# Layer 1's rotation in a two-layer transformer kernel: one sine product over 128 partitions, the halves exchanged by DMAs, additions some rows later

## What is computed

```python
def rope(x):                                  # x: head, token, 128 features
    x2 = x.reshape(*x.shape[:-1], 64, 2)
    rot = jnp.stack([-x2[..., 1], x2[..., 0]], axis=-1).reshape(x.shape)
    return x * cos + rot * sin
q, k, v = xn @ Wq, xn @ Wk, xn @ Wv           # split into heads
q, k = rope(q), rope(k)
scores = (q @ k.T + alibi) / sqrt(128)
scores = 30 * tanh(scores / 30)
probs = softmax(where(causal, scores, -inf))
out = concat_heads(probs @ v) @ Wo + bo
```

## Time and profile before

| | |
|---|---|
| runs | 869.60, 869.14, 864.97 us; median 869.14 |
| the profiled execution | 866.74 us, its span 865.0 us |
| busy | TensorE 779.7 us, VectorE 612.7, ScalarE 465.6, POOL 422.8 |
| layer 1's attention | from about 330 to 706 us of the span |
| DMA | 59.81 MB, most of it on SP's queue |

### The profile page before, as it was taken

How to read it: one execution, slowest core, us unless ns; L and a number is a source line. 1 busy time by engine, 2 the same in 40 slices (tenths; PEclk the granted TensorE clock), 3 DMA queues, 4 the chain that set the end, 5 groups by cost and what they waited for, 6 DMA issues and landing times.

```text
span 865.0 us, 13854 instructions
## 1 busy us (share of the span) xinstructions
PE 779.7 (90%) x4835; PEld 635.0 (73%) x4835; DVE 612.7 (71%) x1063; ACT 465.6 (54%) x819; POOL 422.8 (49%) x478
## 2 busy tenths in 40 slices
PE   2999999988788758898999899999999999999996
PEld 2876776764223237687988788989999999988884
DVE  8388869547988868788877886767766654445555
ACT  3433342259888823676645556556566555655431
POOL 2566846423554454454433357577663412665430
PEclk9999999998989988999999999999999999999999
DMA  5111186000000040000000001110110569644107
GB/s 180 38 53 57 38 243 179 1 1 1 1 1 2 1 143 6 26 7 7 25 7 13 7 26 50 44 37 32 56 50 1 197 128 346 218 146 106 48 4 241
DMA packets 50115, 59.81 MB, mean 69 GB/s; under 512 B 13559, under 2 KB 41084, under 8 KB 50048
## 3 DMA queue, kind: packets, MB, share of 16 engines
q1 hardware_dynamic: 45488, 50.49, 19.2%
q0 software_dynamic: 4560, 8.44, 2.7%
HBM read 41.11 MB, written 21.86 MB: 73 GB/s over the span
## 4 chain that ended last, share of the span: by engine, by line
PE 56%; DVE 12%; POOL 6%; ACT 6%; issue 4%; DMA 1%; POOLq 0%; ACTq 0%; DVEq 0%; SPq 0%
PE ps L771 12%; PE ps L515 8%; PE ps L517 7%; PE ps L516 7%; PE ps L864 4%; PE ps L861 3%; PE ps L895 3%; POOL A L1735 2%; DVE cap L1442 2%; DVE swap L1432 2%; PE ps L609 2%; PE ps L554 2%; PE ps L843 2%; PE ps L686 2%; PE ps L780 1%
## 5 line engine op out<-in xcount | busy, mean ns | idle before, releaser
L1105 ACT ACTIVATE cap<-cap 128x1024 f32<-128x1024 f32 (+7 forms) x128 | 87.1, 680 | 123.1 <-DVE cap L1442 123.1
L771 PE MATMUL ps<-V,P 128*128 128x129 f32 x1152 | 152.6, 279 | 0.0
L771 PEld LDWEIGHTS ps<-V,P 128*128 128x128 f32 x1152 | 145.2, 194 | 2.7
L1442 DVE SCALAR_TENSOR_TENSOR cap<-dist,ps 128x1024 f32<-128x1024 f32 (+7 forms) x128 | 95.1, 749 | 26.2 <-PE ps L517 21.4
L1661 POOL TENSOR_SCALAR_AFFINE_SELECT P<-P 128x128 f32<-128x128 f32 x128 | 38.6, 301 | 148.8 <-ACT P L1110 148.5
L1791 POOL DMA_INDIRECT y_scratch<-y_sb,aux_s x63 | 62.0, 984 | 61.6 <-ACT y_sb L1150 40.3
L1110 ACT ACTIVATE P<-cap 128x1024 f32<-128x1024 f32 (+7 forms) x128 | 87.7, 685 | 4.1
L515 PE MATMUL ps<-q_hi,k_hi 128*128 128x512 f32 x192 | 72.1, 376 | 6.9 <-DVE cap L1442 6.2
L517 PE MATMUL ps<-q_lo,k_hi 128*128 128x512 f32 x192 | 67.0, 349 | 0.0
L516 PE MATMUL ps<-q_hi,k_lo 128*128 128x512 f32 x192 | 66.8, 348 | 0.0
L1766 POOL TENSOR_TENSOR rot<-rot,swap 128x512 f32<-128x512 f32 x40 | 52.1, 1304 | 19.7 <-DVE swap L1432 19.5
(11 more groups left out here) (288 smaller groups left out, 2099.2 us busy)
## 6 DMA issues: line engine op xcount, KB each, us to landing
xg_scratch<-blank SPq DMA_DIRECT2D x1, 8127.0 KB, 32.5
xa<-xg_scratch SPq DMA_DIRECT2D x63, 128.0 KB, 2.2
ew<-in_experts SPq DMA_DIRECT2D x3, 1920.0 KB, 8.7
y<-y_scratch SPq DMA_DIRECT2D x8, 512.0 KB, 5.4
pk<-in_packed SPq DMA_DIRECT2D x8, 384.0 KB, 3.2
pks<-in_scales SPq DMA_DIRECT2D x8, 384.0 KB, 4.0
ew<-in_experts SPq DMA_DIRECT2D x1, 3072.0 KB, 12.9
wqk<-in_wqk SPq DMA_DIRECT2D x20, 128.0 KB, 2.0
```

What stands on the lines that cost most here:

```text
L771: last = pe.matmul(ps[:, 4 + r % 2, o:o + D1 + 1], P1[:, h % 2, a:a + P], V1[:, j, h // REP, :], start=(j == 0), stop=(j == t))
L1105: act.activation(cap[:, n % 2, 0:w], cap[:, n % 2, 0:w], ACT.Tanh, scale=1.0 / (CAP * float(D1) ** 0.5))\
L1442: dve.scalar_tensor_tensor(out=cap[:, n % 2, 0:w], in0=dist[:, 0:w], scalar=slope, in1=psf[:, 1024 * (n % 2):1024 * (n % 2) + w], op0=ALU. ...
```

## The change

VectorE multiplies the whole bank with the sine in one instruction over 128 partitions, into a new tile sines with one buffer. SP copies its two halves crosswise into swap by two DMAs within SBUF; the semaphores swapped0 and swapped1 count them. A product waits until the exchange before it has read sines; POOL's addition waits for the exchange. In VectorE's program the wait for pj_rot is gone; SP waits for it instead. Outside the start, POOL's addition now comes one row after the projection's row, ScalarE's copy (with the split of wqk) two rows and POOL's subtraction three rows after it. SP loads wqk a projection earlier, between the exchanges, and wo has one buffer. One semaphore (table_ready) is folded into another.

```diff
+        sines = sb("sines", [P, HALF])
...
-        wo = sb("wo", [P, 2, PAIR, D])
+        wo = sb("wo", [P, PAIR, D])
...
+            def load_wqk(n):
+                if n < len(PROJ):
                     sp.wait_ge(wqk_ready, n - 1)
                     sp.dma_start(wqk[:, n % 2], wqk_in[n]).then_inc(in_wqk[n % 2], 16)
+
+            def load_wo(m):
+                if m >= 1:
+                    sp.wait_ge(wo_ready, m)
...
+            def exchange(i):
+
+                sp.wait_ge(pj_cos, i + 1)
+                if i >= 2:
+                    sp.wait_ge(pj_rot, i - 1)
+                for to, frm in ((slice(0, 64), slice(64, 128)), (slice(64, 128), slice(0, 64))):
+                    sp.dma_start(swap[to, i % 2, :], sines[frm, :]).then_inc(swapped[i % 2], 16)
+
+            load_wqk(2)
+            for n, (kind, i) in enumerate(PROJ):
+                exchange(2 * n)
+                exchange(2 * n + 1)
+                load_wqk(n + 3)
                 if kind == "q" and i % PAIR == 0 and i >= PAIR:
                     load_wo(i // PAIR - 1)
...
-                if i >= 2:
-                    dve.wait_ge(pj_rot, i - 1)
                 dve.tensor_tensor(rot[:, k % 3], b, cos1[:, tk], ALU.mult)
-                for to, frm in ((slice(0, 64), slice(64, 128)), (slice(64, 128), slice(0, 64))):
-                    last = dve.tensor_tensor(swap[to, i % 2, :], b[frm, :], sin1[frm, tk], ALU.mult)
-                last.then_inc(pj_cos, 1)
+                if i >= 1:
+                    dve.wait_ge(swapped[(i - 1) % 2], 32 * ((i - 1) // 2 + 1))
+                dve.tensor_tensor(sines[:], b, sin1[:, tk], ALU.mult).then_inc(pj_cos, 1)
...
                 pool.wait_ge(pj_cos, i + 1)
+                pool.wait_ge(swapped[i % 2], 32 * (i // 2 + 1))
                 pool.tensor_tensor(r, r, swap[:, i % 2, :], ALU.add).then_inc(pj_rot, 1)
...
+    rows_later = {"act": (0, 2), "dve": (0, 0), "pool": (1, 3)}[engine]
...
+            now = n < first_row or engine == "dve"
+            out += [x for _, x in todo if now]
+            pending += [x for x in todo if not now]
```

More of the change, by code:

```diff
@@ L361, in build_program @@
         in_pk, in_l1c = [sem("in_pk0"), sem("in_pk1")], sem("in_l1c")
-        in_wqk, in_wo, in_wv = [sem("in_wqk0"), sem("in_wqk1")], [sem("in_wo0"), sem("in_wo1")], sem("in_wv")
+        in_wqk, in_wo, in_wv = [sem("in_wqk0"), sem("in_wqk1")], sem("in_wo"), sem("in_wv")
         in_router = sem("in_router")
@@ L401, in build_program @@
         fT_ready, f_ps, fth_ready, x_ready = sem("fT_ready"), sem("f_ps"), sem("fth_ready"), sem("x_ready")
-        table_ready = sem("table_ready")
+        swapped = [sem("swapped0"), sem("swapped1")]
         mixed, shift_ready = sem("mixed"), sem("shift_ready")
@@ L466, in load_rows @@
                 sp.dma_start(rows_of(b), xg_dram[b * P:(b + 1) * P, 0:D]).then_inc(in_xg[b % NT], 16)
[L468 to L475, removed]
+            def load_wqk(n):
+                if n < len(PROJ):
                     sp.wait_ge(wqk_ready, n - 1)
                     sp.dma_start(wqk[:, n % 2], wqk_in[n]).then_inc(in_wqk[n % 2], 16)
+            def load_wo(m):
+                if m >= 1:
+                    sp.wait_ge(wo_ready, m)
+                sp.dma_start(wo[:], wo_in[m * PAIR * D1:(m + 1) * PAIR * D1, :].rearrange("(h p) n -> p h n", p=P))\
+                    .then_inc(in_wo, 16)
+            def exchange(i):
[9 more added lines that the diff above has]
+                load_wqk(n + 3)
                 if kind == "q" and i % PAIR == 0 and i >= PAIR:
@@ L974, in _ @@
             act.wait_ge(consts_ready, 1)
-            act.activation(ln_sd[:, 0:1], consts[:, 0:1], ACT.Sqrt).then_inc(table_ready, 1)
-            act.wait_ge(table_ready, 1)
+            act.activation(ln_sd[:, 0:1], consts[:, 0:1], ACT.Sqrt).then_inc(act_step, 1)
+            act.wait_ge(act_step, 1)
             act.wait_ge(in_const, 32)
@@ L1084, in split_wo @@
             def split_wo(m):
-                act.wait_ge(in_wo[m % 2], 16 * (m // 2 + 1))
+                act.wait_ge(in_wo, 16 * (m + 1))
                 if m >= 1:
                     act.wait_ge(s_ps, NT * m)
-                act.activation(wo_hi[:], wo[:, m % 2], ACT.Copy).then_inc(wo_hi_ready, 1)
+                act.activation(wo_hi[:], wo[:], ACT.Copy).then_inc(wo_hi_ready, 1)
             def project_part(n, half):
@@ L1106, in scores @@
                     .then_inc(act_step, 1)
-                act.wait_ge(act_step, n + 1)
+                act.wait_ge(act_step, n + 2)
                 if j == 0 and h >= 2:
@@ L1758, in split_wo @@
                 pool.wait_ge(wo_hi_ready, m + 1)
-                pool.tensor_tensor(wo_lo[:], wo[:, m % 2], wo_hi[:].bitcast(F32), ALU.subtract).then_inc(wo_ready, 1)
+                pool.tensor_tensor(wo_lo[:], wo[:], wo_hi[:].bitcast(F32), ALU.subtract).then_inc(wo_ready, 1)
             def project(n, half):
@@ L1863, in follow @@
 def follow(engine):
-    out, later = [], []
+    out, later, pending = [], [], []
+    first_row = next(n for n, s in enumerate(STEPS1) if s[0] == "scores")
+    rows_later = {"act": (0, 2), "dve": (0, 0), "pool": (1, 3)}[engine]
     for n, s in enumerate(STEPS1):
@@ L1873, in follow @@
             out.append(s)
+            pending = [(rows - 1, x) for rows, x in pending]
+            out += [x for rows, x in pending if rows <= 0]
+            pending = [(rows, x) for rows, x in pending if rows > 0]
             if engine in ROUTER and NT * s[1] + s[2] in ROUTER[engine]:
@@ L1888, in follow @@
         elif name == "project":
+            todo = []
             if engine != "act":
-                out.append(s)
+                todo.append((rows_later[0], s))
             if engine != "dve":
-                later.append(("project_part", *s[1:]))
+                todo.append((rows_later[1], ("project_part", *s[1:])))
                 if s[2] == 1 and s[1] + 2 < len(PROJ):
-                    later.append(("split_wqk", s[1] + 2))
+                    todo.append((rows_later[1], ("split_wqk", s[1] + 2)))
+            now = n < first_row or engine == "dve"
+            out += [x for _, x in todo if now]
+            pending += [x for x in todo if not now]
         elif name == "moe":
```

## The result

| | before | after |
|---|---|---|
| median of the runs (8 each) | 868.18 us | 875.24 us (872.04 to 879.75) |
| ratio | 1 | **1.0092**, 95% interval 1.0065 to 1.0118 |
| the profiled execution, its span | 866.74, 865.0 us | 876.26, 874.5 us |
| layer 1's attention: transpositions of its input to the first score row / from there to head 15's | 23.2 / 341.8 us | 26.5 / 346.7 us |

The change makes the kernel slower by 0.9%, 7 us; the prediction said 860, and its range ended at 875. Nearly all of it lies in the attention: 3.3 us at its start and 4.9 us in its heads. The heads that lose most, from first score row to first score row, are 10 (27.6 us for 24.8), 2 (27.8 for 25.6) and 0 (17.4 for 16.0); head 10 has no stall of VectorE at all.

What follows compares the result with a forecast made beforehand. TensorE bounds the kernel, held up by pauses behind VectorE in layer 1's attention, heads 0 to 9. Saved 11.2, less 2.2, 0.8 and 1.0, makes 7.2 us off 866.74: 859.5, given as 860, whole range 849 to 875.

Steps and rivals of the forecast that it cites:

- What goes: VectorE's rotation: 40 sine products on 128 partitions replace 80 on 64, taking away 27.5 us of its work.
- What is saved: Layer 1's attention, heads 0 to 9: 11.2 us in all after stalls, including 2.4 in heads 7 and 9.
- 0.69 us a projection, up to the excess: Early heads: each projection saves 0.69 us, less stalls, at most the head's excess over its length without pauses.
- The 2.4 us for heads 7 and 9: Pauses of 0.70 and 1.70 us go, as ScalarE's copy comes a row later, behind the next tanh and exponential.
- (1) The stalls: VectorE, one sines buffer: waiting for the 2.8 us exchange stalls it 1.1 us where behind, 0.4 where TensorE paces it.
- (2) The start: Before the first score row: exchanges lengthen POOL's rounds, +2.2 us, plus 0.8 for an even chance of slow clock.
- (3) The late low parts: Ends of heads 2, 6 and 10: POOL's subtraction, three rows behind, comes late, about 0.4 us each, 1.0 in all.
- What cost nothing: Single wo buffer free; last wo load delays the expert loads some 5 us, still 20 us before the attention ends.
- Slower, through the exchange: Rival, chance 0.17: exchange takes 4.4 us, start +8.3, stalls some 1 us a head in heads 0 to 5; 878 us.
- All of it comes back: Rival, chance 0.13: exchange at its low end, VectorE never stalls in the attention; 16 us off, 850.
- A wash: Rival, chance 0.22: exchange takes 3.4 us, stalls of 1.7, 4.3 lost at the start; under 2 off, 865 us.
- What would have shown it wrong: Signs: sines waiting over 1.5 us a time, first scores after 353, TensorE waiting for q_lo at over three heads' starts.

Runs made afterwards that it cites:

- e11: The change with first four products made without DMA, POOL's subtraction two rows behind, second sines buffer overwriting part of x_tok: 860.79 us, 0.9906 of the kernel before.
- e8: The change with the first four products made without DMA and POOL's subtraction two rows behind instead of three: 869.71 us, 1.0033 of the kernel before.
- e12: The change with first four products without DMA, subtraction two rows behind, second sines buffer in s_tok until product 14, nothing overwritten: 862.63 us, 0.9946 of before.
- e3: The change with only the first four products, before the first score row, made as before without DMA: 874.96 us, 1.0069 of the kernel before.
- e4: The kernel before with one sine product of 128 partitions straight into swap, halves not exchanged, old order kept: 0.993 of the kernel before.
- e2: The kernel before with only the change's later order of ScalarE's and POOL's parts, two sine products, no exchange: 1.0137 of the kernel before.
- e1: The change with the old order of ScalarE's and POOL's parts, exchange by DMA kept: 1.0101 of the kernel before.
- e5: The change with POOL's subtraction two rows behind its projection instead of three: 1.0097 of the kernel before.
- e6: The change with a second sines buffer, laid over part of the residual x_tok, which it overwrites: 870.32 us, 1.0037 of the kernel before.

## Why the prediction was wrong

**What goes: right.** 27.5 us of VectorE's work were to go; the group went from 55.1 to 27.4.

**The sum, term by term.** The prediction nets the stalls out of its 11.2 us. Taken apart (an estimate: 0.69 us a product in heads 0, 1, 2, 3 and 5, less what it counts there), they are 4.7 us, and the saving ahead of them 15.9. The runs' column is in shares of 868 us; it takes the rungs in the ladder's order, rounded one by one.

| term | forecast | in the runs |
|---|---|---|
| saved, before stalls | -15.9 | -8.2 (e11) |
| stalls at the one sines buffer | +4.7 | +11.0 (e11 to e8; the 7.6 from e12 to e8 are clear of the intervals, the rest is not) |
| late low parts | +1.0 | +3.1 (e8 to e3) |
| the start, slow clock included | +3.0 | +2.0 (e3 to after) |
| together | -7.2 | +8.0 |

So the two steps that failed are the saving, 7.7 us too large, and the price of the stalls, 6.3 too small; the late parts come third, with 2.1.

**What is saved: too large.** The run without exchange and without stalls (e4) shortens all heads by 341.8 - 334.5 = 7.3 us and heads 0 to 6 by 5.3, where the prediction had 8.8 in heads 0 to 6 even after its stalls. The step that failed is "0.69 us a projection, up to the excess". It holds in head 2, where e4 saves the forecast 1.1 us and 3.07 us of the longest pause stay, and fails in heads 1, 4 and 6: after its stalls the forecast has 2.3 (slow clock included), 1.5 and 2.0 there, and e4 saves 0.8, 0.1 and 0.4. In head 6 TensorE waits for VectorE's additions to s_tok, and three products of 128 partitions for six don't shorten that: 0.58 and 2.09 us before, 0.93 and 1.75 in e4.

```profile
491.15 0.39 PE L515 MATMUL ps<-wo_hi,cT_hi 128*128 128x256 f32 x1 [0.58 <-DVE s_tok L1471]
...
502.57 0.38 PE L515 MATMUL ps<-wo_hi,cT_hi 128*128 128x256 f32 x1 [2.09 <-DVE s_tok L1471]
```

```profile
485.39 0.38 PE L515 MATMUL ps<-wo_hi,cT_hi 128*128 128x256 f32 x1 [0.93 <-DVE s_tok L1469]
...
496.44 0.38 PE L515 MATMUL ps<-wo_hi,cT_hi 128*128 128x256 f32 x1 [1.75 <-DVE s_tok L1469]
```

The prediction took the whole difference between a head and its length without pauses as VectorE's rotation work coming late. Why head 4 gives only 0.1 isn't taken apart.

The 2.4 us for heads 7 and 9 came in half. Both pauses are gone, and head 7 takes 19.0 us for 20.0, but head 9 takes 22.7 for 22.6: at its end VectorE waits 2.97 us for the sends (587.08), and TensorE 1.59 for VectorE (until 588.74). The prediction asked what ended the pause, and not what would end next: the last send lands where it did in the head before, and VectorE, some 2 us earlier, can't go on without it.

**(1) The stalls: the size nearly right, the price too low.** The exchange is 2.9 us where 2.8 was taken, and of the eleven stalls within the heads nine have 0.39 to 0.90 us, about the forecast 0.4 to 1.1. Two, in heads 1 and 2, have 2.06 and 1.84, since those exchanges took 4.6 and 4.3 us. The 11 stalls make 9.8 us; with the second buffer until head 4 (e12) they fall from e8's 9.9 to 3.7, 6.2 us less, and the heads get 343.7 - 335.3 = 8.4 us shorter (7.6 by the ratios). All of it lies in heads 0 to 3. So once the low parts are in time a stall of VectorE there costs about all that it takes; whether more is within what single profiles differ by. How is argued, not tried apart: the score row is queued behind it, and tanh, the exponential and POOL's mask behind that, and the slow clock after a pause adds to it.

**(2) The start: right.** +2.2 us was forecast, +3.3 measured (26.5 against 23.2), and the first score's matmul waits 2.66 us for q_lo, as the chain said. But 0.8 of the 3.3 us lie ahead of the first product, where the programs do the same: the first cosine product starts 5.43 us behind the first transposition before and 6.27 after, with the granted clock at its low level in after. The windows of before and of after, from the first projection on:

```profile
330.20:332.50 2.30, 2.30 (x11) 1.80 (x10) 1.88 (x5) 0.63 (x2) 0.00 (x0) 0.85 0.00 0
```

```profile
332.00:334.30 2.30, 2.30 (x8) 1.82 (x7) 1.60 (x4) 0.60 (x1) 0.00 (x0) 0.50 0.00 0
```

From that cosine product to the first score row it is 17.79 us before and 20.19 after, **+2.4**: 2.2 until POOL's first addition, and 0.2 in the rounds. In the seven other kernels that start with two products (e2, e3, e8 to e12) it is 17.78 to 17.81, and in e1, e5 and e6, which start as the change does, 19.89 to 20.86.

**(3) The late low parts: 1.0 us forecast, 3.1 by the ladder.** "About 0.4 each, 1.0 us in all", in heads 2, 6 and 10. There are five waits, 8.2 us (10.8 less the start's 2.66), at the ends of heads 0, 1, 2, 6 and 10. The prediction priced one subtraction by its own delay behind one mask. But in POOL's queue the moved additions and subtractions stand behind one another, behind the split of wqk and of wo and, in head 10, the sends; and in head 2 they wait together for a mask whose score row is late on VectorE, behind the router's run and a stall of 1.84 us (403.43). The order alone shows them in e2: 8.3 us in four waits behind the start's, and 1.4% of time. By the ladder only 3.1 of the 8.2 us are time lost; without these waits TensorE waits 5.3 us more for VectorE's cap (e5).

**What cost nothing: right.** The first load of experts is issued at 698.20 us for 679.41, so 18.8 us later, where "some 5" was said (10 of them are the attention's own lateness). From head 15's first score row to the end of the span it is 172.8 us, before 173.2.

**The clock.** The granted clock from 350 to 400 us is 0.93 as before, at more pauses; in the 4 us from 424 on, behind the wait at 422.04, it is 0.67 (windows of after), which is the low level, 1.2 GHz, for two thirds of them. The 0.8 us allowed for the start didn't come: in the 4 us behind that wait the clock is 1.00. Of the five later waits for q_lo three have low clock behind them (0.50 in the 4 us from 369.40, 0.67 from 424, 0.59 from 613.70), two have none (1.00 from 394.50 and from 521.80).

**The rivals.** "Slower, through the exchange" had the direction and nearly the time (878), but by 4.4 us of exchange, and with a turning point at 3.6. The exchange takes 2.9 us, and the change loses at that. Its places were right as well (the start, and stalls in the first heads), but it needed 8.3 us at the start and has 2.4. "All of it comes back" asked for 16 us; even e4 and e11, without a stall, are 6 and 8 below the kernel before. "A wash" took 1.0 us for the heads' ends like the forecast, and falls with it. The rule of the Trainium skill's page SBUF — State Buffer ("Can I just issue two DMAs to hit both halves?") gave 3.3 us by an estimate; this case's trace has 2.9, which is an issue, 0.56, and a landing, 2.3. The trace doesn't decide whether the two transfers follow each other, as the rule says, for the second issue alone sets it 0.56 us behind the first.

**What would have shown it wrong** did: sines waiting over 1.5 us a time (three times: at 339.05, 381.34 and 403.43), first scores after 353 (353.32), q_lo waited for at more than three heads' starts (five).

## What to carry to other kernels

An engine's work moved to where it "has time" is paid at the deadline: before moving a chain of small parts some rows later, list all that its queue holds up to the moment when the next stage needs the last of them, and price the queue, not the part. Where a pause is to go, ask what ends just before it: in head 9 the sends took its place, and in head 6 the additions to s_tok had made it all along. A DMA that replaces 0.7 us of an engine's work brings a round trip of 2.9 us and wants a second buffer on its source side: with the two smaller repairs alone the kernel lost 0.3%, with the buffer as well it gained 0.5%. And where several waits stand behind one another, repairing one may show little in the time, so look at whether the wait moved before calling the theory dead.

## What the hardware showed unasked

- Two DMAs within SBUF of 64 x 512 floats, crosswise, take 2.86 to 2.93 us from the end of the product to the release of its tile in eleven of the 14 cases in which VectorE waited for them, 3.36 in one, and 4.58 and 4.31 in heads 1 and 2. Those two were issued without delay (376.79 and 399.15, 0.03 us behind their products). In e3 and e8 the same places give 4.60, 4.22 and 4.17, 4.61. What holds these up was not tried. The DMA view of each of the six from the product's end to the release has one transfer on an instruction queue (q8, 0.02 MB), that of the other twelve in the change has none; that the two go together is shown, that one delays the other is not.
- SP needs 0.559 us to issue one of them, against 0.328 for the load of wqk.
- 9.4 MB more traffic (36 exchanges of 2 x 128 KB) beside the attention cost TensorE nothing that shows: heads 11 to 14 take the same in e11, with it, and in e4, without, to 0.01 us.
